# A state-space scan with routed experts on one core: prologue and end re-ordered, half of dt ahead of the routing

## What is computed

```python
xn = layernorm(x)                                   # the first norm
# state-space part
xs = layernorm(xn) * norm_w + norm_b                # the second norm
delta, B, C = split(xs @ x_proj_w.T)                # 128 | 64 | 64
dt = softplus(delta @ dt_proj_w.T + dt_proj_b)      # (tokens, 256)
h[t] = exp(dt * A) * h[t-1] + dt * B * xs           # 256 channels x 64 states
y = (h * C_used).sum(states)                        # C_used: C of token t % 64
out1 = (y + xn * D_param) @ out_proj_w.T
# expert part
shared = relu2(xn @ w_up) @ w_down                  # 512 wide
top 6 of 64 experts per token (8 groups, 4 kept), weights from sigmoid scores
out2 = shared + sum over the 6: w * (relu2(xn @ w1[e]) @ w2[e])
return x + out1 + out2
```

## Time and profile before

| | |
|---|---|
| median of 3 runs | 1054.94 us (1049.82 to 1057.08) |
| the profiled execution's own time | 1047.24 us |
| its span | 1045.5 us |
| first scan starts | 226.98 us |
| block 1 (tile 32) starts | 335.57 us |
| block 7 starts | about 852.1 us |
| last scan ends | about 1003.5 us |
| busy: VectorE, TensorE, GpSimd, ScalarE | 923.7, 726.6, 578.1, 544.6 us |

### The profile page before, as it was taken

The page is one execution under the profiler, slowest core; times in us unless marked ns, Lnnn a source line. Parts: engine busy times, 40 slices in busy tenths (PEclk is TensorE's granted clock), DMA queues, the critical chain, the costliest instruction groups (busy, mean ns, idle before and its releaser), DMA issues. The chain is left out here.

```text
span 1045.5 us, 18790 instructions
## 1 busy us (share of the span) xinstructions
PE 726.6 (70%) x6663; PEld 454.5 (43%) x6664; DVE 923.7 (88%) x842; ACT 544.6 (52%) x807; POOL 578.1 (55%) x391
## 2 busy tenths in 40 slices
PE   1868683014556988989988999988999875333336
PEld 1835352001222655656655666665665542111125
DVE  6579976889999999999999999999999999999963
ACT  0204054543334777877878777877787853221200
POOL 5001147777503656667676666757676675777710
PEclk9679897555555899999999999999998975555557
DMA  9990004693222999999999999999999963433332
GB/s 333 354 342 23 0 26 165 226 307 116 89 53 69 263 277 286 287 286 286 291 290 292 275 264 288 283 262 285 299 286 277 268 189 99 108 101 98 99 110 80
DMA packets 178653, 217.83 MB, mean 208 GB/s; under 512 B 50433, under 2 KB 137858, under 8 KB 178306
## 3 DMA queue, kind: packets, MB, share of 16 engines
q1 hardware_dynamic: 169346, 191.45, 64.9%
q0 software_dynamic: 9216, 25.18, 7.7%
HBM read 144.61 MB, written 71.83 MB: 207 GB/s over the span
## 5 line engine op out<-in xcount | busy, mean ns | idle before, releaser
L962 DVE TENSOR_TENSOR_SCAN H<-ps,U 128x1024 f32<-128x1024 f32 x256 | 581.2, 2283 | 25.6 <-ACT ps L687 21.7
L687 ACT ACTIVATE ps<-ps,Acur 128x1024 f32<-128x1024 f32 x256 | 278.9, 1090 | 242.0 <-PE ps L1126 240.5
L591 POOL TENSOR_TENSOR U<-X,B 128x1024 f32<-128x1024 f32 x100 | 237.5, 2375 | 198.4 <-DVE H L962 141.7
L1126 PE MATMUL ps<-PK,sel 24*128 24x512 bf16 x824 | 162.3, 447 | 222.4 <-DVE H L962 145.2
L1115 PE MATMUL ps<-H,CB 128*32 128x128 f32 x4096 | 240.9, 395 | 5.7 <-DVE H L962 5.7
L1126 PEld LDWEIGHTS ps<-PK,sel 24*128 24x128 bf16 x824 | 45.2, 93 | 332.1 <-issue 292.2
L1115 PEld LDWEIGHTS ps<-H,CB 128*32 128x32 f32 x4096 | 143.2, 130 | 85.8 <-issue 26.5
L591 POOL TENSOR_TENSOR U<-GS,B 128x1024 f32<-128x1024 f32 x50 | 120.0, 2401 | 28.5 <-DVE H L962 24.6
L621 POOL DMA_INDIRECT WE<-yg_d,slot x96 | 93.8, 977 | 41.5 <-issue 22.4
L577 POOL DMA_INDIRECT xg_d<-XN,slot x96 | 98.7, 1028 | 30.0 <-issue 28.8
L1210 PE MATMUL ps<-WE,AS 128*128 128x256 f32 x320 | 95.4, 423 | 0.0
(11 more groups left out here) (146 smaller groups left out, 615.9 us busy)
## 6 DMA issues: line engine op xcount, KB each, us to landing
X<-g_d SPq DMA_DIRECT2D x200, 256.0 KB, 6.3
WE<-w_exp_dram SPq DMA_DIRECT2D x160, 256.0 KB, 5.0
xg_d<-CB SPq DMA_DIRECT2D x20, 1024.0 KB, 11.2
XG<-xg_d SPq DMA_DIRECT2D x80, 256.0 KB, 6.6
yg_d<-YO SPq DMA_DIRECT2D x80, 256.0 KB, 6.3
PK<-pk_d SPq DMA_DIRECT2D x64, 128.0 KB, 6.3
pk_d<-GS SPq DMA_DIRECT2D x16, 256.0 KB, 3.8
X<-x_dram SPq DMA_DIRECT2D x4, 512.0 KB, 5.6
```

The lines of the kernel that those rows point to most:

```text
L591: nc.gpsimd.tensor_tensor(U[:, c % 4, :], rows, B2[:, b * L:(b + 1) * L], ALU.mult).then_inc(u_pool, 1)
L687: nc.scalar.activation(a_tile(c), a_tile(c), ACT.Exp, scale=Acur[:, b, pair:pair + 1]).then_inc(a_ready, 1)
L962: V.tensor_tensor_scan(H[:, (s // GRP % 2) * GRP + s % GRP, :], a_tile(s), U[:, s % 4, :], 0.0, ALU.mult, ALU.add).then_inc(scan_done, 1)
L1126: return mm(ps[:, bank, :], sel[32 * g:32 * g + ROWS, c % SUB, :], PK[32 * g:32 * g + ROWS, c // SUB % NPK, :], start=True, stop=True)
```

## The change

1. **One norm's statistics.** The second norm's variance is worked out from the first's (v / (v + eps)); one root serves both; ScalarE writes XN2 = XN * scale. The statistics of x start with its first quarter. Jobs are by group of four token tiles.
2. **Half of dt ahead.** After the transposes come dpre and dt of rounds 0 and 1, their softplus and split, and only then logits and routing. Rounds 2 and 3 stand behind the routing. Two rounds are interleaved step by step, with buffers of their own. The product g and both differences of its split are GpSimd's (g_split).
3. **Routing.** GpSimd makes the six products OH * scores and three of the six OH * positions; VectorE keeps the sums. ScalarE evacuates B and prefix. GpSimd's list behind "slot" is 8 scatters, then g_split of rounds 2 and 3 with 3 scatters between, adds, 33 scatters, adds, 40 scatters; the last 12 (DEFER) stand amid its products in the first 16 tiles of block 1.
4. **Shared expert.** D_param goes into the weights (dwo) and is applied by two more products in each of the 16 down steps. 12 steps stand ahead of prefix, 14 behind dt, and 6 in block 0, in tiles 0 to 10.
5. **Pairs.** FIRST = 8, REST = 14: the first 8 slots are free, then every 14th. SP waits for all scatters at tile 12 of block 1 and there issues the first three pairs' 9 DMAs.
6. **End.** y is loaded in four parts, three of them during block 7; ScalarE re-orders it (turn); the projection runs over 7 banks, with the first halves of tiles 8 to 14 ahead of the second; the sum goes into XN, from where it is stored.

```diff
-REST = 7
+REST = 14
+FIRST = 8
+DEFER = 12
+        JOBS = ([(kind, 2 * g + h, who) for g in range(4) for kind, who in (("xn2T", "dve"), ("xnT", "act")) for h in range(2)]
+                + [("dpre", q, "act") for q in range(3)] + [("dt", q, "dve") for q in range(2)]
+                + [("dpre", 3, "act")] + [("dt", q, "dve") for q in range(2, 4)]
+                + [("logit", q, "act") for q in range(2)] + [("B", q, "act") for q in range(4)]
+                + [("C", q, "dve") for q in range(2)]
+                + [("prefix", q, "act") for q in range(4)] + [("dt", q, "dve") for q in range(4, 8)])
+        SH_FIRST, SH_LAST = 12, 26
...
@@ sync
+                    if it == 0 and s == 20:
+                        sp.wait_ge(sh_ready, TT)
+                        sp.dma_start(xs_d.rearrange("(k p) d -> p k d", p=P), X[:, :, :]).then_inc(xs_stored, 16)
+                    if it == PRE and s == 2 * FIRST - 4:
+                        sp.wait_ge(scattered, 16 * TT * TOPK)
+                        for p in range(MBUF):
+                            load_inputs(p)
+                            load_weights(experts_of(p), p)
...
@@ gpsimd
+                    i = it * SL + c - NPRE
+                    if 0 <= i < 4 * (DEFER // 3) and i % 4 != 2:
+                        scatter(TT * TOPK - DEFER + i // 4 * 3 + min(i % 4, 2))
+            def g_split(q, stage):
+                h, b = q // 2, q % 2
+                if stage == 0:
+                    pool.wait_ge(dt_done, q + 1)
+                    nc.gpsimd.tensor_tensor(l_t[b], z_t[b], xn2T[:, h, b * L:(b + 1) * L], ALU.mult).then_inc(g_done, 1)
+                elif stage == 1:
+                    pool.wait_ge(first_g, q + 1)
+                    nc.gpsimd.tensor_tensor(u_t[b], l_t[b], prt3[b][:, 2, :], ALU.subtract).then_inc(rest_g, 1)
+                else:
+                    pool.wait_ge(second_g, q + 1)
+                    nc.gpsimd.tensor_tensor(prt[b][:, 1, :], u_t[b], prt3[b][:, 3, :], ALU.subtract).then_inc(split_g, 1)
+            def weight(k):
+                pool.wait_ge(oh_ready, k + 1)
+                if k >= 2:
+                    pool.wait_ge(wn_summed, k - 1)
+                nc.gpsimd.tensor_tensor(weighted[k % 2], OH[k], sc, ALU.mult).then_inc(oh_sc, 1)
+            def position(k):
+                pool.wait_ge(pos_ready, 1)
+                pool.wait_ge(wn_summed, TOPK)
+                nc.gpsimd.tensor_tensor(weighted[k // 2], OH[k], pos, ALU.mult).then_inc(oh_pos, 1)
...
@@ scalar, behind dpre
+            exp_of(0)
+            exp_of(1)
+            log_of_one_plus(0)
+            log_of_one_plus(1)
+            first_part(0, 0)
+            first_part(1, 0)
+            first_part(0, 1)
+            second_part(0, 0)
+            first_part(1, 1)
+            second_part(1, 0)
+            second_part(0, 1)
+            second_part(1, 1)
...
@@ vector
+            steps_of_two(0)
+            dve.wait_ge(act_evac, evac_no(JN["logit", 1]))
...
+            for k in range(TOPK):
+                dve.wait_ge(oh_sc, k + 1)
+                V.tensor_reduce(wn[:, :, k], t64(weighted[k % 2]), AX.X, ALU.add).then_inc(wn_summed, 1)
...
+            steps_of_two(1)
+            dve.wait_ge(split_t, 4)
+            dve.wait_ge(g_done, 4)
```

More of the change, by code:

```diff
@@ L370, in _, with store_zeros @@
             zr = xg_d.rearrange("(a p) d -> p a d", p=P)
[L371 to L374, removed]
+            zeros = CB[:, :, :, :].rearrange("p b r m -> p (b r m)")[:, 0:8 * D].rearrange("p (a d) -> p a d", d=D)
+            def store_zeros(first, last):
+                for c in range(first, last):
+                    sp.dma_start(zr[:, 8 * c:8 * c + 8, :], zeros).then_inc(zeros_stored, 16)
             pad = pk_d.rearrange("s (c g a) t -> (s c) g a t", g=4, a=4)
@@ L405, in load_g, with store_parts @@
                         .then_inc(s_gs[dma_slot(c)], 16)
-            for q in range(4):
+            def store_parts(q, kind, split):
                 h, b = q // 2, q % 2
[L409 to L429, removed]
@@ L737, in _ @@
             evac_group(BLK * 4 - 1, 1)
+            act.wait_ge(s_y[3], 32)
+            for c in (0, 8):
+                turn(1, 1, c, c + 8)
         @block.vector
@@ L788, in _ @@
[L788 removed]
+            for k in range(TT):
+                if k % 4 == 0:
+                    dve.wait_ge(s_x[k // 4], 16)
+                ins = V.bn_stats(st6[:, k, :], X[:, k, :])
+                if k == TT - 1:
+                    link(ins)
+            for k in range(TT):
+                ins = V.bn_aggr(mv[:, k, :], st6[:, k, :])
+            link(ins)
+            link(V.tensor_scalar(rtmp[:, 0, :], mv[:, :, 1], EPS, None, ALU.add))
@@ new lines, in _ @@
+            steps_of_two(0)
+            dve.wait_ge(act_evac, evac_no(JN["logit", 1]))
+            dve.wait_ge(bias_in, 16)
+            dve.wait_ge(consts, 6)
+            dve.wait_ge(split_t, 2)
+            dve.wait_ge(g_done, 2)
+            t8 = lambda a: a.rearrange("p (g e) -> p g e", e=8)
+            t64 = lambda a: a.rearrange("p (t e) -> p t e", e=EXPERTS)
+            g1, g2, g3, gs, pen = (small[:, 128 * n:128 * n + 128] for n in range(5))
+            link(V.tensor_scalar(sc, sc, 1.0, None, ALU.add))
@@ L1100, in _ @@
                 ins.then_inc(job_done, 1)
+            for s in range(SH_FIRST, SH_LAST):
+                shared_step(s)
             pe.wait_ge(dve_evac, evac_no(JN["dt", 7]))
-            pe.wait_ge(act_evac, evac_no(JN["dpre", 3]))
+            pe.wait_ge(up_sq, 4 * (SH_LAST // 8) + SH_LAST % 8)
             def y_rows(F, s, first, last):
```

549 lines of the change are left out of this document (326 added, 223 removed).

## The result

The changed kernel takes 1014.34 us (median of four runs, 1002.4 to 1017.7) against 1055.06 for the kernel before. The two runs of 1017.5 and 1017.7 count as slow, over 1.5% above the fastest, so the ratio goes by the other two, whose mean is 1006.8: it is 0.955, with a 95% interval of 0.946 to 0.964. That is **faster, and 1014 as well as 1007 lies within the range given**. The profiled execution took 1002.40 us with a span of 1000.67.

What follows compares the result with a forecast made beforehand. VectorE was taken to bound blocks 0 to 7, a serial chain with waits the prologue; -39.5 (prologue) + 3 (block 0) + 7 (blocks 1 to 6) + 0 - 17 (end) = -46.5, from 1054.94 to 1008 us, range 985 to 1025.

Steps and rivals of the forecast that it cites:

- First scan: End of prologue: first scan at 187.5 us instead of 226.98, a gain of 39.5.
- second pass: Prologue reckoning with GpSimd and VectorE blocking each other, each waiting its turn in full: first scan at 187.5.
- first pass: Prologue reckoning with free ports: first scan at 167, gain 60; as a rival, 988 us in all, chance 0.13.
- the OH products on GpSimd give nothing: Routing in the prologue: wn complete 24.4 us after the first OH, about what VectorE alone took before.
- Charging the loop nothing for the port: Loop: VectorE instructions with one SBUF input outside 2-port modes don't contend with GpSimd, so no cost.
- The prologue's TensorE at 1.2 GHz: Rival, prologue: dpre and dt at the low clock, 11 us more before the second z; 1019 us, chance 0.14.
- Block 0: Shared down steps on TensorE delay the spreading of dt and g: +3 us, bounds 0 and 10.
- Blocks 1 to 6: Loop: 2.5 us through GpSimd's lead, about 4.5 from late g rows at tile 20; +7, bounds 0 and 12.
- later slots: +0: Loop's later slots: a slot with a pair takes 5.51 us in both kernels, so no added cost.
- the loop becomes DMA's: Rival, loop: dense pairs exceed the DMA rate, 80 slots cost 20 us more; 1025 us, chance 0.18.
- The +7 of the first tiles: Block 1's early tiles: GpSimd's products and scatters, then SP's wait delaying g rows of tile 20; bounds 0 and 12.
- End: After the last scan's end E: finish at E + 24.3 instead of 42.0; 17 us gain taken, bounds 3 and 18.

Runs made afterwards that it cites:

- e4: Changed kernel with the product g and its two differences back on VectorE for all four rounds; 998.2 us, first scan at 175.49.
- e6: Changed kernel with the routing's nine products (six with scores, three with positions) back on VectorE; 1015.2 us, first scan at 182.01.
- after: The changed kernel itself with no further edit; its profiled execution took 1002.4 us, with a loop (blocks 1 to 6) of 530.5.
- e1: Kernel before the change with only the pairs' slots moved (start at slot 8, rest every 14th); 1054.6 us.
- e2: Changed kernel loading only the first half of each expert's weights (256 of 512 columns), engine instructions unchanged; 986.0 us.
- e8: e4 with pairs from slot 2, a rest every 8th slot and no deferred scatters; 1091.2 us, ratio 0.971, where the kernel before took 1122.9.
- e13: The kernel of e8 again on another chip; median 990.5 us, ratio 0.940 to the kernel before.
- e3: Changed kernel with SP's wait for the scatters and the nine DMAs moved behind its other loads of the same iteration; 1011.1 us.
- e9: Changed kernel with four buffers for the experts' weights instead of three, loads asked for a pair earlier; 1005.9 us.
- e0: Changed kernel run again with no edit, to see how far two executions differ; 1011.7 us.

## Why the prediction was right, and where it wasn't

*Total.* 1008 forecast, 1014 measured (1006.8 by the runs in the ratio); for the profiled execution -46.5 forecast, and -43.4 + 2.6 + 13.9 + 0.2 - 18.1 = -44.8 found. That the total is so near is luck in part: the prologue gave 3.9 more than forecast and the end 1.1, which made up for most of the 6.9 that the loop cost more. The mechanism of prologue, block 0 and end was the one forecast; in the loop two of its terms were wrong.

*First scan* 187.5, found 181.8 to 183.6. The second pass, in which each port conflict is paid in full, was the right one; the first pass (167) is refuted by the trace and by e4 and e6, which put work on VectorE and lose nothing. The statement that the OH products on GpSimd give nothing held to within a microsecond (e6: 182.01 against 181.89; from the first z, whose start differs, 148.20 against 148.87). What I didn't see is that the same holds more strongly of g: I took the split for part of a gain, and it is 8 us of loss, since each link waits for an operation more than twice as long (3.1 to 3.4 us against 1.22). Of the 3.9 us too many, 2.2 stood at slot (the OH phase took 22.1 us to wn complete where I had 24.4) and 1.4 more came in the second half of dt (VectorE done at 173.2, forecast 176.8). Scalar operations and a cast were lengthened too (133.38: 2.06 us, 64.77: 2.18), which I had charged nothing. What the Trainium skill says (SBUF — State Buffer, Who interferes with whom) is borne out for two-input operations: 3.25 us instead of 1.23. The same section lists copies, casts and scalar operations among those that can take the shared ports in a 2-port mode; I had used only the half that speaks of operations outside these modes. Charging the loop nothing for the port was right: all 256 scans of after took 2.26 to 2.29 us, those beside GpSimd's products too.

*The prologue's TensorE at 1.2 GHz.* Right to be a rival, and right that it didn't come: four products of 512 columns took 1.88 at 33.25, the rate of 15.49 for 32.

*Block 0* +3, found +2.6: the up to 1.9 us more per down step came (the one at 200.69 took 4.5 where I had put 2.6 at the full clock and 5.2 at the low one), and one of them shows as a stall of 2.9 at tile 11. The 2.6 for six products doesn't follow from the row it names: the earlier trace rows has 1.10 for four records, which makes 3.3 for twelve.

*Blocks 1 to 6* +7, found +13.9, by several runs some +11 to +18. The step that failed is "later slots: +0", which rested on a slot with a pair taking 5.51 in both kernels; tiles 64 to 223 took 11.7 us more than before. Most single slots still take that; what grew is the number of slots over 6 us, from 6 to 9 in these tiles, and the longest of them, from 6.8 to 8.3. A dense row of slots isn't the sum of single ones, as the rival "the loop becomes DMA's" said. In e1 the pairs' slots alone make these tiles as long as in after. Less the 2.5 us or so of the six pairs that were only moved there, some 9 are left, about half of that rival's 20: more of the loop's loss came by its way than by the forecast's. (Its total was mis-added: 1008 and 20 are 1028, not 1025, and lie outside the range.) A rate and not a mean duration had to be costed; e2 gives 16 to 25 back by bytes alone. How much of it is the density stays open (e8, e13).

The +7 of the first tiles was wrong too. Tiles 32 to 47, where 2.5 us were to come through GpSimd's lead, took 41.4 us where before they took 43.3; tiles 48 to 63 took 47.8 where 43.6. Together that is +2.3, with the stall of 5.2 in it. The stall came at the tile and in the size forecast, but by another carrier: I had named the rows of g, it was the load of the parts of dt and g, eight tiles ahead in SP's order. That its size fitted is luck. e3 removes it, and tiles 32 to 63 are 5.5 us shorter; whether the total keeps them, one run can't show.

*Block 7* 0, found +0.2. *End* E + 24.3, found E + 23.9: 14.08 for the 64 products where 14.4 stood (the 0.9 for four records isn't in the earlier trace rows either, whose four took 1.10; 14.08 makes it 0.88); y arrived in time, and the one gap of 3.0 us in VectorE's additions (994.60) cost nothing, since TensorE had none.

## What to carry to other kernels

Where two engines take turns at a port, as these two did, an elementwise step moved from the busy one to the idle one can gain nothing (e6) and costs where it is a link of a chain (e4, 8 us): its length stands on both. When work that needs the queues is packed denser, cost it by bytes per time over the dense stretch, not by the duration of one slot: a small lateness is hidden and many aren't. A stall that is removed (e3) or a buffer that is added (e9) need not show in the total where the queues behind it are full: look whether the lateness turns up elsewhere. And split a stage before explaining it: in e1 the loop as a whole hid a gain of 4 and a loss of 12.

## What the hardware showed that I had not expected

- The turns are taken by small operations too: beside GpSimd's products, scalar operations and a cast of VectorE of 2 to 64 elements per partition took 1.78 to 2.06 us instead of 0.17 to 0.26 (133.38 above, against 130.44 of e6), and one of 1024 elements 2.18 instead of 0.70 (64.77, against e4's 61.53).
- On one chip of several, the kernel before took 1122.9 us instead of 1051 to 1055, and TensorE, VectorE and ScalarE of e8 stood for up to 35, 34 and 30 us in block 0, while indirect DMAs were issued; the loop, which has none in e8, ran as elsewhere (530.2 us).
- Two executions of the same changed kernel (e0) differ by 9.3 us, all of it in the loop; the end took 23.9 in both and block 7 151.5 and 151.3. In tiles 160 to 191 the same 25.7 MB (289 GB/s for 89.0 us, 269 for 95.8) took 6.7 us longer in e0, with the DMA engines 0.98 busy instead of 1.05.
